# The decay gates of a linear-attention block computed in rows instead of columns

## What is computed

```python
h = layernorm(x) * (1 + ca) + sa
q = elu(h @ Wq) + 1 ; k = elu(h @ Wk) + 1 ; v = h @ Wv          # 16 heads of 64
a = sigmoid(h @ Wa + ba + 2.0)                                   # one decay for each token and head
S = a_t * S + k_t v_t^T ;  z = a_t * z + k_t                     # scan over the tokens
out = (q_t S) / (q_t z + 1e-6) ;  x = x + ga * (out @ Wo)
```

## Time and profile before

| | before |
|---|---|
| median of 3 runs | 3454.72 us (3454.70 to 3460.96) |
| the profiled execution | 3456.77 us, of which the span is 3455.0 us |
| busy | PE 94%, PE weight loads 80%, DVE 75%, ACT 53%, POOL 41% |
| attention phase | to about 2600 us of the span; the experts follow |
| granted TensorE clock, mean | 0.985 |

### The profile page before, as it was taken

One profiled execution on the slowest core, in us unless ns is written; L12 is line 12 of the kernel. 1 busy time (PEld: TensorE's weight loads), 2 busy tenths in 40 slices (PEclk: granted clock), 3 DMA queues, 4 the chain that ended last, 5 costly groups with the idle time before them and its releaser, 6 DMA issues. The chain is left out here.

```text
span 3455.0 us, 130112 instructions
## 1 busy us (share of the span) xinstructions
PE 3259.2 (94%) x51114; PEld 2754.8 (80%) x51114; DVE 2604.3 (75%) x6738; ACT 1816.2 (53%) x4493; POOL 1425.9 (41%) x1122
## 2 busy tenths in 40 slices
PE   6999999999999999999999999999986999999999
PEld 5888888888887887888888888888875777777777
DVE  5777877777777877787777778787755788778786
ACT  4666666666666665666666666666632222322321
POOL 4444444545444444445454444444431222222222
PEclk9999999999999999999999999999987999999999
DMA  4222222222222222222222322222212111111110
GB/s 139 76 76 74 74 82 71 80 72 73 81 87 77 74 77 72 75 73 78 75 73 77 92 74 73 77 77 76 70 42 80 44 44 38 50 38 38 46 41 25
DMA packets 158635, 238.79 MB, mean 69 GB/s; under 512 B 30232, under 2 KB 82504, under 8 KB 157768
## 3 DMA queue, kind: packets, MB, share of 16 engines
q1 hardware_dynamic: 158024, 230.33, 21.1%
HBM read 194.58 MB, written 35.67 MB: 67 GB/s over the span
## 5 line engine op out<-in xcount | busy, mean ns | idle before, releaser
L447 POOL TENSOR_TENSOR qs_sb<-lam_bc,qk_sb 128x512 f32<-128x512 f32 x256 | 521.7, 2038 | 1150.3 <-DVE qk_sb L931 976.8
L550 ACT ACTIVATE kd_sb<-bank_scores,decay 128x64 f32<-128x64 f32 x2048 | 448.0, 330 | 290.3 <-PE bank_scores L803 283.4
L916 DVE SCALAR_TENSOR_TENSOR s_mid<-s_mid,lam_bc,bank_dense 128x65 f32<-128x65 f32 x1536 | 433.3, 282 | 55.9 <-DVE s_mid L916 1.3
L455 POOL TENSOR_TENSOR oT_lo<-oT,oT_hi 128x512 fp32r<-128x512 f32 x256 | 328.4, 1283 | 84.1 <-ACT oT_hi L527 83.8
L510 ACT ACTIVATE qk_sb<-bank 128x512 f32<-128x512 f32 x512 | 316.7, 619 | 70.7 <-PE bank L589 56.3
L512 ACT ACTIVATE qk_sb<-qk_sb 128x512 f32<-128x512 f32 x512 | 323.3, 632 | 16.3
L587 PE MATMUL bank<-wv_hi,h_hi 128*128 128x256 f32 x1024 | 307.7, 300 | 24.9 <-DVE qk_sb L929 11.0
L966 DVE TENSOR_TENSOR p_sb<-bank_scores,decay 128x512 f32<-128x512 f32 x256 | 176.1, 688 | 190.5 <-ACT kd_sb L550 188.7
L937 DVE TENSOR_TENSOR_SCAN decay<-a_bc,eye 128x512 f32<-128x512 f32 x256 | 310.9, 1214 | 1.3 <-DMA a_bc<-rows_dram 1.3
L1292 DVE SCALAR_TENSOR_TENSOR acc<-bank,comb,acc 128x256 f32<-128x256 f32 x512 | 229.6, 475 | 103.0 <-ACT acc L1160 93.4
L803 PE MATMUL bank_scores<-qk_sb 64*64 64x128 f32 x8192 | 288.1, 276 | 13.8 <-ACT oT_hi L527 4.3
(11 more groups left out here) (204 smaller groups left out, 8795.9 us busy)
## 6 DMA issues: line engine op xcount, KB each, us to landing
a_bc<-rows_dram SPq DMA_DIRECT2D x512, 128.0 KB, 3.1
lam_bc<-rows_dram SPq DMA_DIRECT2D x512, 128.0 KB
x_in<-in_L_attn_x_dram SPq DMA_DIRECT2D x32, 512.0 KB, 5.0
x_res<-in_L_attn_x_dram SPq DMA_DIRECT2D x32, 512.0 KB, 3.9
x_dram<-x_res SPq DMA_DIRECT2D x32, 512.0 KB, 2.9
x<-x_dram SPq DMA_DIRECT2D x32, 512.0 KB, 3.3
out_dram<-x SPq DMA_DIRECT2D x32, 512.0 KB, 2.9
ew_raw<-in_L_ffn_expert_W_dram SPq DMA_DIRECT2D x8, 256.0 KB, 5.7
```

The costliest lines, as they stand in the source:

```text
L447: pool.tensor_tensor(qs_sb[:, na, :], lam_bc[na][:, :], q_sb, ALU.mult).then_inc(qs_ready, 1)
L455: pool.tensor_tensor(oT_lo[:, u, :], oT32[:, :], oT_hi[:, u, :].bitcast(F32), ALU.subtract).then_inc(oT_lo_ready, 1)
L550: ins = act.activation(kd_sb[:, t, hd * DH:(hd + 1) * DH], KTR[:, hd, t * CK:(t + 1) * CK], ACT.Copy, scale=decay[:, hd, t, CK - 1:CK])
L916: dve.scalar_tensor_tensor(dst, src, lam_bc[nb][:, (ch + 1) * CK - 1:(ch + 1) * CK], U[ch], ALU.mult, ALU.add).then_inc(state_step, 1)
```

## The change

The gates are computed with heads on partitions from the start. Wa is the weight (its 16 columns twice, `REP` = 2, so that a matmul fills 32 partitions), the tokens move, 128 columns at once; the four quarters of a group (first or second chunk of a 128-token block f, first or second half of the group th) go to the four 32-partition strips of Q. ACT takes the exponential out of PSUM with the bias of each partition. DVE does the rest in one go at the end of step 2, and scans 128 columns on 128 partitions. Job "a" is gone. The rows lie in another order, so that the stores are 13 DMAs instead of 7, and they are issued in step 3 instead of step 4.

```diff
-              (2, 1): ("z", 1, 0), (3, 0): ("v", 1, 1), (3, 1): ("a", 1, 0), (4, 0): ("v", 1, 2), (5, 0): ("v", 1, 3),
+              (2, 1): ("z", 1, 0), (3, 0): ("v", 1, 1), (4, 0): ("v", 1, 2), (5, 0): ("v", 1, 3),
@@ SP: loads at the start
-            sp.dma_start(ba_raw[:, :], ba.partition_broadcast(128)).then_inc(small_loaded, 16)
-            sp.dma_start(wa[:, :, :], Wa.rearrange("(k p) n -> p k n", p=128)).then_inc(small_loaded, 16)
+            for at in range(0, 128, HEADS):
+                sp.dma_start(ba_raw[at:at + HEADS, :], ba.rearrange("(h o) -> h o", o=1)).then_inc(small_loaded, 16)
+            for at in range(0, REP * HEADS, HEADS):
+                sp.dma_start(wa[:, :, at:at + HEADS], Wa.rearrange("(k p) n -> p k n", p=128)).then_inc(small_loaded, 16)
@@ SP: store_rows, 5 + 2 DMAs become 9 + 4
                 sp.wait_ge(a_row_ready, T + 1)
+                for f in range(2):
+                    for th in range(2):
+                        at, to = quarter(f, th), slice(th * CH, (th + 1) * CH)
+                        sp.dma_start(a_dst[:, f, to], a_rows[at:at + HEADS:2, :]).then_inc(rows_stored, 16)
...
                 sp.wait_ge(lam_row_ready, T + 1)
+                for f in range(2):
+                    for th in range(2):
+                        at = quarter(f, th)
+                        sp.dma_start(lam_dst[:, 2 * th:2 * th + 2, f, :],
+                                     lam_rows[at:at + HEADS, :].rearrange("r (t i) -> r t i", t=2)).then_inc(rows_stored, 16)
                 sp.wait_ge(rows_stored, (T + 1) * 16 * ROW_STORES)
...
-                if u == 4 and exists(T + 1):
+                if u == 3 and exists(T + 1):
                     store_rows(T + 1, 1 - s)
@@ ACT
-                if job == "a":
-                    act.wait_ge(arow_ps, of + 1)
-                    after(act, rows_stored, of * 16 * ROW_STORES)
-                    act.activation(a_row[:, :], Q[0:HEADS, :], ACT.Copy).then_inc(a_row_ready, 1)
+                if job == "z":
+                    act.wait_ge(z_ps, of + 1)
+                    act.wait_ge(ba_ready, 1)
+                    after(act, a_step, of * 3)
+                    act.activation(a_exp[:, :], Q[:, 0:GT // 4], ACT.Exp, bias=neg_ba[:, 0:1], scale=-1.0).then_inc(z_exp, 1)
...
-                if u == 2 and exists(T + 1):
-                    act.wait_ge(zb_ready, T + 2)
-                    act.activation(a_tok[:, :, :], a_tok[:, :, :], ACT.Exp, scale=-1.0).then_inc(z_exp, 1)
@@ PE: q_bank_free
                 if u == 3 and exists(T + 1):
-                    pe.wait_ge(zb_ready, T + 2)
-                if u == 4 and exists(T + 1):
-                    pe.wait_ge(a_row_ready, T + 2)
-                    pe.wait_ge(lam_row_ready, T + 2)
+                    pe.wait_ge(z_exp, T + 2)
@@ PE: z_job (arow_job is gone)
-                for ch in range(NCH):
-                    for kt in range(KT):
-                        for at in range(0, CH, SLICE):
-                            mm = pe.matmul(Q[at:at + SLICE, ch * HEADS:(ch + 1) * HEADS],
-                                           h32[:, kt, ch * CH + at:ch * CH + at + SLICE],
-                                           wa[:, kt, :].rearrange("p (q h) -> p h q", h=2),
-                                           start=(kt == 0), stop=(kt == KT - 1))
+                for kt in range(KT):
+                    h_tok = h32[:, kt, :].rearrange("p (t f i) -> p t f i", t=NCH, f=2)
+                    for f in range(2):
+                        for th in range(2):
+                            at = quarter(f, th)
+                            mm = pe.matmul(Q[at:at + REP * HEADS, 0:GT // 4].rearrange("p (t i) -> p t i", t=2), wa[:, kt, :],
+                                           h_tok[:, 2 * th:2 * th + 2, f, :], start=(kt == 0), stop=(kt == KT - 1))
@@ DVE: z_out, sigmoid_step and decay_products become decay_rows, called in step 2 after p_sb
+            def decay_rows(T):
+                firsts = [t[:, :].rearrange("p (t i) -> p t i", t=2)[:, :, 0:1] for t in (a_first, a_rows)]
+                dve.wait_ge(z_exp, T + 1)
+                dve.tensor_scalar(a_exp[:, :], a_exp[:, :], 1.0, None, ALU.add).then_inc(a_step, 1)
+                after(dve, rows_stored, T * 16 * ROW_STORES)
+                dve.wait_ge(a_step, T * 3 + 1)
+                dve.reciprocal(a_rows[:, :], a_exp[:, :]).then_inc(a_step, 1)
+                dve.wait_ge(a_zero, 1)
+                dve.wait_ge(a_step, T * 3 + 2)
+                dve.tensor_copy(firsts[0], firsts[1]).then_inc(a_step, 1)
+                dve.wait_ge(a_step, T * 3 + 3)
+                dve.memset(firsts[1], 0.0).then_inc(a_row_ready, 1)
+                dve.wait_ge(a_row_ready, T + 1)
+                dve.tensor_tensor_scan(lam_rows[:, :], a_rows[:, :], a_first[:, :], 0.0, ALU.mult, ALU.add).then_inc(lam_row_ready, 1)
```

More of the change, by code:

```diff
@@ L269, in attention_phase, with quarter @@
         SPLIT_AT = {0: (WQ,), 1: (WV,), 3: (WK,), 4: (WO0, WO1)}
-        SMALL = 3
+        SMALL = 1 + (4 + 1) * REP
         MOD_A = 4
-        ROW_STORES = 7
+        ROW_STORES = 13
         SECTION = [0, 1, 3, 4]
+        def quarter(f, th):
+            return (f * 2 + th) * REP * HEADS
         def place(hd, ch):
@@ L321, in store_rows @@
             def store_rows(T, sT):
-                dst = rows_dram[sT, 0].rearrange("q f (h t i) -> h f q t i", h=2, t=NCH)
+                a_dst = rows_dram[sT, 0]
+                lam_dst = rows_dram[sT, 1].rearrange("q h n -> (q h) n").rearrange("r (t f i) -> r t f i", t=NCH, f=2)
+                half = GT // 2
                 sp.wait_ge(a_row_ready, T + 1)
-                src = [a_row[hd * PAIRS:(hd + 1) * PAIRS, :].rearrange("r (t f i) -> r t f i", f=2, i=CK) for hd in range(2)]
-                sp.dma_start(dst[0, 0], src[0][:, :, 0, :]).then_inc(rows_stored, 16)
@@ new lines, in store_rows @@
+                for th in range(2):
+                    at, to = quarter(1, th) + 1, slice(half + th * CH, half + (th + 1) * CH)
+                    sp.dma_start(a_dst[:, 0, to], a_rows[at:at + HEADS - 1:2, :]).then_inc(rows_stored, 16)
+                at = quarter(0, 1) + 1
+                sp.dma_start(a_dst[:, 1, half + CK:half + 3 * CK], a_rows[at:at + HEADS - 1:2, :]).then_inc(rows_stored, 16)
+                at = quarter(0, 0) + 1
+                sp.dma_start(a_dst[:, 1, half:half + CK], a_rows[at:at + HEADS - 1:2, CK:2 * CK]).then_inc(rows_stored, 16)
@@ L396, in _ @@
             pool.memset(neg_bound[:, :], 0.0).then_inc(fills, 1)
-            pool.memset(first[:, :], 0.0).then_inc(fills, 1)
-            pool.memset(later[:, :], 1.0).then_inc(fills, 1)
             pool.memset(half_neg[:, :], -0.5).then_inc(consts_ready, 1)
-            pool.wait_ge(fills, 6)
+            pool.wait_ge(fills, 4)
             pool.memset(bound[:, :].rearrange("p (r e) -> p r e", e=2)[:, :, 1:2], BIG).then_inc(consts_ready, 1)
@@ L822, in _ @@
                .then_inc(siluT_ready, 1)
-            dve.wait_ge(consts_ready, 7)
-            dve.memset(a_cols[:, :, :], 0.0)
+            dve.wait_ge(consts_ready, 5)
+            dve.memset(a_first[:, :], 0.0).then_inc(a_zero, 1)
             def split_weight(n):
```

89 lines of the change are left out of this document (21 added, 68 removed).

## The result

The changed kernel takes 3509.74 us at the median (3499.30 to 3517.63, four runs); the kernel before, on the same chip, 3455.08 (3454.70 to 3460.96). The ratio is 1.0158, with a 95% interval of 1.0144 to 1.0172: 55 us slower, where 45 us less had been forecast, and outside the range. The profiled execution of the changed kernel took 3499.30 us, 42.5 more than that of before.

The account below looks back on a forecast made before the run. PE, busy 94%, was taken as the bound, with wq's wait for DVE's scan in step 4 standing out. Group gains of 7.2, 17.4, 6 and 18 make 48.6, less 3 for the start: 3410 us forecast, range 3388 to 3441.

Parts of the forecast that it names:

- the term of SP's stores: SP, step 3: 13 stores at 0.34 us with gap take 4.5 us ahead of the loads; costed at nothing.
- The cover of 0.5 us: Step 4, even groups: a_bc lands at 1530.65, the scan wants it at 1531.15, so 0.5 us to spare.
- Rival (B): Stores at 0.55 us each make a_bc of step 3 the bound: 3483 us; chance 0.06, its milder form 0.07.
- The landing: SP, step 3: 1.33 us from the end of the last store to the next load.
- The gains: Plain even groups 1.8 us, half-clock ones 2.9, other even ones 1.0, odd ones 1.2; together 48.6 us.
- PE's wait for L885: Step 4: wq waits for DVE's scan, 25.0 us over 23 waits; the change takes this wait away.
- The z job: PE, step 2: 16 passes of 128 columns replace 64 of 16; no change, near 0.7 us, bounds -0.2 and +1.2.
- rival (A): The z job's strips don't run at once, making it 1.2 us longer: 3439 us; chance 0.08.
- DVE's end of step 2: Added work of 1.95 us about offsets what is removed; step 2 comes out even, 0.1 us gained, bounds +0.4 and -0.3.
- Rival (C): DVE's addition in step 2 costs more, or PE's "issue" stalls move: half the gain, 3433 us; chance 0.11.
- The start: Prelude: eight more DMAs ahead of the loads of wmod, for which PE waits; 3 us lost, once.
- The granted clock: Step 4 of groups 6, 8, 18 to 24: half clock was to become 1.00.

Follow-up runs that it names:

- e1_contig: Changed kernel, but the nine stores of a_rows read eight neighbouring partitions (half the rows belong to other heads): 3423.09 us, ratio 0.9905 to the kernel before.
- e3_order: Changed kernel, but in step 3 SP issues the a_bc loads, then the 13 stores, then lam_bc, and waits for their landing in step 4: 3396.78 us, ratio 0.9834.
- e7_norecip: e3_order with the reciprocal of the gates replaced by one multiply-and-add that gives 0.9: 3378.89 us, ratio 0.9779 to the kernel before.
- e5_probe: e3_order plus fourteen stores of a constant tile behind the attention's last store, differing in partition pitch, rows or columns: 3409.03 us, one run.
- e4_nostore: Changed kernel without the thirteen stores from group 2 on, so later groups use old rows: 3416.52 us, ratio 0.9899 to the kernel before.
- e8_contig: e3_order with Wa's columns ordered even heads, then odd, so stores read neighbouring partitions and carry the right rows: 3413.28 us, ratio 0.9886 to the kernel before.
- e10_order_again: The same instructions as e3_order, run again as a yardstick: 3394.10 us, ratio 0.9828 to the kernel before.
- e6_contig_order: e3_order with Wa's columns ordered as in e8_contig and the loads of ba and Wa behind the big weights': 3412.38 us, ratio 0.9882 to the kernel before.

## Why the prediction was wrong, point by point

**The step that failed: the term of SP's stores, put at 4.5 us and therefore at no cost.** "A store takes 0.31 us, with its gap 0.34; 13 are 4.5." The row is of stores that read eight neighbouring partitions, and the new ones don't: nine pick every second one. They measured 0.65 with the gap, and the four of lam, on sixteen neighbouring partitions, 0.46: 7.8 us for the thirteen, so that the loads of step 3 go out 9.0 us after the first store and not 5.9. The cover of 0.5 us was gone, and DVE waits 3.1 us for `a_bc` in even groups and 4.2 in odd ones. e1_contig shows that this one term decides the sign: with the price of the row for the nine the kernel is 1% faster, with the real price 1.6% slower. The other half of the step, that the stage is covered, failed too: at the row's price the odd groups still wait 1.5 us, and e1_contig is 25 us above e3_order (0.9905 less 0.9834). The measured time of e1_contig, 3423 us, would have been inside the range. Rival (B) had the mechanism, its price (0.55 against a measured mean of 0.60 with gaps) and the point from which it decides (0.47). I gave it 0.06 and argued against it with the four pieces a row of the old stores, which is a form of the destination; the form of the source had no row. The trace of before held a hint that I used for the rival and not for the sum: `a_bc`'s loads, also of another form, take 0.55. A step without a row of its own form should have had the bounds 0.34 and 0.55 in the sum, and then the range would have held both signs.

**The size of (B).** 3483 against 3510. Even groups came out better than it said (0.7 us gained, where it let all groups lose, 0.8 in the mean), odd ones much worse (3.8 us lost). The odd ones were the weak spot of the argument: I wrote that they come "about 0.4 late, where DVE has as much slack". In them step 3 is shorter (6.85 us against 7.98, no clamp), so the scan wants `a_bc` 1.1 us sooner; at the real price that is 4.16 us late, and step 4 grows by 4.05: there was next to no slack. Even groups were helped by something I had not known: the clamp took 0.29 us in step 4 of all thirteen, and 1.2 in that step before (below).

**The landing.** 1.2 us after the last store (1563.66 to 1564.85), 1.33 in the prediction, so the loss didn't come from there. The Trainium skill ("DMA: Bandwidth & Descriptors", Anatomy of one DMA) has about 2.0 for the fixed part, but of a DMA that GpSimd issues; these are issued by SP, and the 1.2 us are only what follows the issue. The two are not the same stretch, and the prediction should not have put one in the other's place; the measurement decides.

**The gains were right, and more than counted.** PE's wait for L885 is gone. In step 3 of group 18 `k_sb` follows `k_sb` after 7.96 us, where I had 8.1 and the kernel before 9.32. With the stores out of the way (e3_order) even groups gain 3.0 us (81.09 to 78.08) and odd ones 0.7 (76.89 to 76.20): I had 1.8 or 2.9 with half clock, 1.0 for the even ones with stalls, and 1.2 for odd. The total, 54 to 59 us in the two runs, is above my 45, but not by the sum that I wrote. Groups 3 to 28 give 48 us of the 58 between the profiled executions of before and e3_order, and about 12 come from group 29 on (9 in the changed kernel), where the sum had some 3; the start takes 2. Single even groups from 4 to 28 gain between 0.1 us and 5.7: seven gain 3 us or more, five about 2, group 4 nothing. Only four of the six to which I gave 2.9 are among the seven. The parts of the sum were right in kind; that the total came near is partly luck.

**The z job.** 0.64 us for 16 passes of 128 columns, I had "near 0.7". One pass takes 273 ns, so that 16 in a row would be 4.4 us: the passes overlap, the price of the strips held, and rival (A) is out. The rule of the Trainium skill ("TensorE: Matmul & The Clock Gate", Part 3: Packing small matmuls), by which a weight load overlaps matmuls in flight only where the row groups differ, would have made it 1.9 us by my estimate. The trace doesn't agree: the 16 weight loads, all on 128 rows, lie within the 0.64 us too. The same section lets a load into the background weight buffer run ahead as well, which the prediction left out.

**DVE's end of step 2.** The reciprocal 0.95 (0.94 foreseen), the scan 0.42 (0.40), the add 0.22 (0.25); `p_sb` of step 2 no longer waits for `kd_sb` in even groups, and 0.49 us in odd ones (0.90 in both before). "Comes out even" held: 10.83 to 10.69 in even groups, 9.74 to 9.95 in odd ones. But PE now waits up to 1.3 us for `k_sb` at its end, and e7_norecip shows that step 2 shortens by as much as DVE's work there. Rival (C) was therefore half right as a bound, and wrong as a loss.

**The start.** 4.0 us (10.16 to 14.18) against 3: the eight loads of ba take 0.45 each with the gap, not 0.37.

**The granted clock.** It did not become 1.00 throughout: from 60 to 2650 us I count 22 stretches at half clock (123 us) after, 14 before (96 us), and 8 in e3_order (55 us). The six behind the waits for L885 went. Of the 20 after, up to 2500 us, 19 stand at a wait of PE for `o_sb` of 2.0 to 5.5 us.

## What to carry to other kernels

A DMA's issue time on its queue depends on its form, and e5_probe hints at the DMA ahead of it too: take it from a row with the same pattern of partitions and a like neighbour, and where there is none, carry both the cheapest and the dearest row of that queue through the sum. When stores go ahead of loads on one queue, ask first whether they can stand behind the load that is waited for: that order was worth 112 us here, and halving the stores' price in the wrong place 87. When work on an engine is removed, everything behind it comes sooner, so the slack of each transfer has to be worked out against the new times, in the shortest kind of group and not in the one that was looked at.

## What the runs showed of the hardware that was not expected

- SP issues a store of eight rows in 0.30 us when they lie on neighbouring partitions and in 0.60 when they lie on every second one, with the same bytes and the same destination (e1_contig against the changed kernel). A pitch of 4 costs no more than one of 2, and half the columns no less (e5_probe).
- The clamp of `carry` (128x65, on DVE) takes 1.21 us at the median and sometimes 0.29, with the same operands, and which of the two it takes goes by whether POOL is inside an instruction when it starts. The twelve traces hold 1440 clamps. 147 started with POOL idle and took 0.29 us. 1285 started inside an instruction of POOL and took 1.19 to 1.34; every one of them ends 47 to 59 ns after that instruction. The other 8 started within 53 ns ahead of one and were long too. Here are POOL and DVE in steps 3 and 4 of group 18 of the changed kernel:

```profile
1557.90 2.13 POOL L457 TENSOR_TENSOR qs_sb<-lam_bc,qk_sb 128x512 f32<-128x512 f32 x1 [6.50 <-DVE qk_sb L908]
...
1570.71 1.27 POOL L457 TENSOR_TENSOR qs_sb<-lam_bc,qk_sb 128x512 f32<-128x512 f32 x1 [9.44 <-DMA lam_bc<-rows_dram]
```

```profile
1558.87 1.21 DVE L880 TENSOR_SCALAR carry<-carry,bound,neg_bound 128x65 f32<-128x65 f32 x1
```

  The clamp of step 4 starts at 1569.99, before POOL's `qs_sb`, and takes 0.29. So a late `lam_bc` has a good side. In step 4 of even groups `qs_sb` starts 6.1 us behind `k_sb` in the changed kernel and 4.0 in e3_order, and there the clamp is short in all 13 groups from 4 to 28. It starts after 2.3, 1.8 and 2.0 us in before, e4_nostore and e8_contig, and the clamp is short in 0, 1 and 3 of them. Over steps 4 and 5 that leaves e3_order 3 us ahead of e4_nostore, and e10_order_again level with e8_contig. This is a reading of traces; no run was made for it.
- PE's long waits on "issue" end 2.1 to 2.9 us after the start of a transfer of instructions (158 of 164, above). Some come at the same instruction in every kernel of the new form (one near PE's 26980th, with 1.3 to 1.6 us), others, such as those in step 6 of groups 6 and 20, only in some. Half clock follows some and not others: with it such a step took 10.6 to 10.7 us in e8_contig, without it 9.2 in e6_contig_order.
